# Attention and routed experts on one core: block loops written out, and three reorderings in the attention part

## What is computed

```python
# x: (2, 1024, 256), ctx: (2, 154, 256)
def attention(q_in, kv):               # 16 heads of 16
    q, k, v = q_in @ Wq + bq, kv @ Wk + bk, kv @ Wv + bv
    scores = q @ k.T / 4 - slope[h] * abs(j - i - (Nk - Nq))
    return softmax(scores) @ v @ Wo + bo
def experts(x):                        # 8 experts, 256 -> 1024 -> 256
    g = softmax(x @ Wg + bg); top2, idx = top_k(g, 2)
    top2 = top2 / (sum(top2) + 1e-8)
    return sum over e of combine[:, e] * (gelu(x @ W1[e] + b1[e]) @ W2[e] + b2[e])
x = x + attention(layernorm(x), ctx)
x = x + experts(layernorm(x))
```

## Time and profile before

| what | us |
|---|---|
| median of three runs (lowest, highest) | 479.41 (478.26, 480.38) |
| the profiled execution's own time | 479.1 |
| its span in the profile | 476.4 |
| PE, DVE, ACT, POOL busy in the span | 411.7, 314.1, 241.7, 196.7 |
| attention and routing, up to the last read of the schedule's start | 219.7 |
| blocks, from the first turned rows to the last add | 224.7 to 476.4 |

### The profile page before, as it was taken

The page is one execution under the profiler, slowest core; times in us unless marked ns, Lnnn a source line. Parts: engine busy times, 40 slices in busy tenths (PEclk is TensorE's granted clock), DMA queues, the critical chain, the costliest instruction groups (busy, mean ns, idle before and its releaser), DMA issues.

```text
span 476.4 us, 16113 instructions
## 1 busy us (share of the span) xinstructions
PE 411.7 (86%) x5037; PEld 321.7 (68%) x5038; DVE 314.1 (66%) x849; ACT 241.7 (51%) x625; POOL 196.7 (41%) x337
## 2 busy tenths in 40 slices
PE   5878898999999999931989999899989997999980
PEld 4656666666777777720867777688758876887760
DVE  6677899999988766454463666466646664666661
ACT  2337677777776556531543454345434453544430
POOL 3202488888777646683022222133212331223231
PEclk9989899999999999975898999899989998999996
DMA  7577677677776542534121331122313221322210
GB/s 262 109 193 231 196 258 216 208 196 220 220 200 205 161 111 73 162 118 147 43 50 25 48 49 35 33 44 37 45 27 56 40 44 26 51 49 29 24 14 0
DMA packets 53977, 50.70 MB, mean 106 GB/s; under 512 B 24353, under 2 KB 47905, under 8 KB 53793
## 3 DMA queue, kind: packets, MB, share of 16 engines
q1 hardware_dynamic: 46152, 41.06, 30.1%
q0 software_dynamic: 7152, 8.47, 10.5%
q10 hardware_dynamic: 624, 0.54, 0.3%
HBM read 33.73 MB, written 17.50 MB: 108 GB/s over the span
## 4 chain that ended last, share of the span: by engine, by line
PE 44%; issue 3%; DMA 3%; DVE 2%; POOL 1%; SPq 0%; ACT 0%; POOLq 0%; DVEq 0%; ACTq 0%
PE ps L1074 43%; PE ps L1310 2%; DMA out<-o,row_id 1%; DMA out<-xn,row_id 1%; DMA xlist<-rows,pos 1%; DMA area<-xlist 0%; POOL out L620 0%; DVE area L1032 0%; DVE xn L1049 0%; POOL xlist L589 0%; ACT area L775 0%; DVE o L1052 0%; DVE area L1030 0%; DVE xn L1052 0%; DVE o L1049 0%
## 5 line engine op out<-in xcount | busy, mean ns | idle before, releaser
L1074 PE MATMUL ps<-area,wts 128*128 128x128 f16 (+1 forms) x2896 | 197.6, 243 | 0.0
L1074 PEld LDWEIGHTS ps<-area,wts 128*128 (+1 forms) x2896 | 158.5, 103 | 41.2 <-issue 2.9
L1074 PE MATMUL ps<-wts,area 128*128 x624 | 154.8, 332 | 1.9 <-DVE area L1032 1.6
L775 ACT ACTIVATE area<-ps,late 128x128 f32<-128x128 f32 x312 | 89.2, 368 | 115.8 <-PE ps L1074 114.5
L1030 DVE TENSOR_SCALAR area<-area 128x512 f16<-128x512 f32 x78 | 33.0, 423 | 79.1 <-ACT area L775 79.0
L1074 PE MATMUL ps<-area 128*128 128x128 f16 (+3 forms) x832 | 66.5, 233 | 4.4 <-DMA area<-qd 2.0
L620 POOL DMA_INDIRECT out<-o,row_id x20 | 31.4, 1572 | 93.6 <-issue 64.4
L620 POOL DMA_INDIRECT out<-xn,row_id x19 | 30.1, 1587 | 94.1 <-issue 81.4
L1074 PEld LDWEIGHTS ps<-area 128*128 128x128 f16 (+1 forms) x832 | 51.0, 102 | 14.5 <-issue 6.4
L646 ACT ACTIVATE area<-ps 128x512 f32<-128x512 f32 x80 | 47.3, 595 | 24.1 <-PE ps L1074 22.3
L872 DVE TENSOR_REDUCE mx<-ps 128x3 f32<-128x462 f32 (+1 forms) x96 | 53.2, 576 | 6.9 <-PE ps L1074 6.6
(11 more groups left out here) (124 smaller groups left out, 432.0 us busy)
## 6 DMA issues: line engine op xcount, KB each, us to landing
stage<-in_w SPq DMA_DIRECT2D x32, 512.0 KB, 4.3
area<-xlist SPq DMA_DIRECT2D x39, 130.0 KB, 2.1
area<-qd SPq DMA_DIRECT2D x16, 256.0 KB, 3.6
qd<-wts SPq DMA_DIRECT2D x48, 64.0 KB, 3.1
area<-in_x SPq DMA_DIRECT2D x16, 128.0 KB, 4.6
out<-area SPq DMA_DIRECT2D x16, 128.0 KB
xlist<-pad_rows SPq DMA_DIRECT2D x11, 130.0 KB, 2.7
area<-in_b SPq DMA_DIRECT2D x1, 1024.0 KB, 6.9
```

Of the source, the lines that this page charges most:

```text
L775: last = nc.scalar.activation(h32[par][:, c * P:(c + 1) * P], h_ps[par][m][:, f * P:(f + 1) * P], ACT.Gelu_apprx_tanh, bias=b1T[:, ds(e * ...
L1074: return nc.tensor.matmul(out_, lhsT, rhs, start=start, stop=stop, skip_group_check=skip)
```

## The change

1. A new helper `straight` writes all block steps out, on all five engines. No loop and no branch is left. Expert numbers are read in longer groups: PE reads 21 values ahead of its first step and 19 between the steps t=19 and t=20; ACT reads 11 at first, then 13 ahead of t=10, 13 ahead of t=22 and 5 ahead of t=34; DVE 10, 12, 12 and 5 at the same places. SP and POOL have plain constants in their waits; the extra semaphore step that each of their waits had in a loop (`wait_alone`) goes.
2. In DVE's turn the residual and its statistics stand ahead of the rest of the turn's first weight unit, and `maxima(sc, 5)` behind the second norm's `bn_aggr`.
3. Routing's negated maximum is computed by ACT, right ahead of the exponential that uses it, no longer by POOL.
4. The rests of the last two weight units (30 and 31), which stood at the ends of turns 16 and 17, stand behind the schedule.

```diff
+        def straight(step, eng, first, ahead=None, most=NBLK):
+            t = first
+            while t < NBLK:
+                n = min(most, NBLK - t)
+                known = None if ahead is None else experts(eng, t, n + ahead)
+                for k in range(n):
+                    step(t + k, (t + k) % 4, *([] if ahead is None else [known[k:]]))
+                t += n
...
-            blocks(lambda t, slot: load_block(t + 4, slot) if not isinstance(t, int) or t + 4 < NBLK else None, sp, -4)
+            straight(lambda t, slot: load_block(t + 4, slot) if t + 4 < NBLK else None, sp, -4)
...
-            def least(t):
-                pool.wait_ge(s.m8_d, t + 1)
-                wait(pool, s.e8_d, t)
-                pool.tensor_scalar(small[:, 0:1], m8[:, 0:1], -1.0, None, ALU.mult).then_inc(s.nm_d, 1)
...
-                    least(b2)
...
-            blocks(add_block, pool, 0)
+            straight(add_block, pool, 0)
...
+                    act.wait_ge(s.m8_d, b2 + 1)
+                    wait(act, s.e8_d, b2)
+                    nc.scalar.activation(small[:, 0:1], m8[:, 0:1], ACT.Copy, scale=-1.0).then_inc(s.nm_d, 1)
                     act.wait_ge(s.nm_d, b2 + 1)
...
-            blocks(step, act, -2, 1)
+            straight(step, act, -2, 1, 12)
...
                     maxima(sc, 4)
-                for u in units[0:1] if i < NT else []:
-                    split_w_lo(u)
                 if b1 is not None:
                     dve.wait_ge(s.pr_ps, b1 + 1)
                     dve.tensor_tensor(xr[:, b1 % 8, :], misc[:, D:2 * D], xr[:, b1 % 8, :], ALU.add).then_inc(s.x2_d, 1)
                     dve.wait_ge(s.x2_d, b1 + 1)
                     dve.bn_stats(st2[:], xr[:, b1 % 8, :]).then_inc(s.st2_d, 1)
-                if sc is not None:
-                    maxima(sc, 5)
+                for u in units[0:1] if i < NT else []:
+                    split_w_lo(u)
                 if b1 is not None:
                     dve.wait_ge(s.st2_d, b1 + 1)
                     wait(dve, s.xn2_d, b1)
                     dve.bn_aggr(mv2[:], st2[:]).then_inc(s.mv2_d, 1)
                 if sc is not None:
+                    maxima(sc, 5)
+                if sc is not None:
                     negated(sc)
-                for u in earlier[1:2] + units[0:1] if i >= NT else []:
-                    split_w_lo(u)
...
             dve.tensor_copy(sched_i[0:1, 1, 0:NBLK], expert[0:1, :]).then_inc(s.sched_done, 1)
+            for u in weight_units(NT):
+                split_w_lo(u)
...
-            blocks(step, dve, -2, 0)
+            straight(step, dve, -2, 0, 12)
...
-            blocks(step, pe, -2, 1, 8)
+            straight(step, pe, -2, 1, 22)
```

## The result

The changed kernel takes 465.83 us (462.7 to 466.13, 4 runs), the kernel before 478.84 beside it (4 runs). The ratio is 0.9726, 95% interval 0.9653 to 0.9799: 2.7% faster, 13 us where 7 were forecast. The profiled execution took 465.93 (span 464.1, against 476.4).

The account below looks back on a forecast made before the run. PE was taken to bound plain block steps, with register reads idling it at loop heads; DVE and POOL paced attention turns. Terms -11.84 + 2.0 + 2.2 + 0.8 = -6.8 took 479.1 to 472.3 us, range 466.5 to 477.5.

Parts of the forecast that it names:

- Loops out: Block stage: 18.55 us of excess at PE's loop heads goes, 6.71 at t=20 comes in its place; -11.84 us.
- Longer reads on ACT and DVE: Block stage: ACT's 13-value reads ahead of t=10 and t=22 delay PE by 1.0 us each; +2.0, bounds 0 and 7.8.
- The residual ahead of the rest: Attention turns: PE's residual wait goes, but POOL's lock ends later and lengthens turns; +2.2 us, bounds -4.2 and +4.8.
- The negated maximum: Attention routing: POOL loses an operation of some 0.2 us, half-idle ACT gains 16 of 0.20; no change, 3.2 without cover.
- The last two rests: Attention's end: schedule done 1.5 us earlier, but PE's read of 21 values delays its first block; +0.8 us.
- the lower bound's case: Start of PE's first block: the load of its rows decides again, not PE's read; -1.5 us instead of +0.8.
- Plain steps of 5.53: Block steps between PE's loop heads: PE, busy throughout, bounds them, and they stay at 5.53 us.
- A: Rival, attention turns: each of eight turns gets shorter by PE's 0.53 us wait; 465.9 us, chance 0.15.
- B: Rival, blocks: the clock falls more often, at ACT's late GELUs and the long read at t=20; up to 478.1 us, chance 0.14.
- C: Rival, instruction supply: written out, each of some 33 formerly looped steps takes 0.13 us more; 476.6 us, chance 0.10.
- D: Rival: long reads cost far more per value, 0.49 us; 489 us, slower by over 0.5% from about 0.39; chance 0.05.

Follow-up runs that it names:

- The two traces compared above: First to last second norm: 157.4 us with the changed order and PE reading in groups of 12, 154.7 in the changed kernel with the residual behind the rest again.
- the run with the blocks alone: Only the written-out blocks, the three other edits undone, against the kernel before: 469.0 us, ratio 0.9715; run again on another chip, 463.45 us, ratio 0.9722.

## Why the prediction was wrong

The direction was right, the size was not: 13 us for 7. By its own steps:

- **Loops out.** The heads' 18.55 went. The price that failed is "19 x 0.242 = 4.60" plus "2.11 for the slow clock and the registers": the step measured 2.05 above 5.53, not 6.71. The read took 1.85, for it starts at number 20; every read that the trace of before had between blocks, with its start at 3, 11, 19, 27 or 35, was of the dear kind, and the one from number 0 met those of ACT and DVE, so the price per value looked constant. The clock did not fall after 1.42 us of idle time. That alone is 4.7 us of the gap. The Trainium skill's 200 ns a register, weighed there, is stated for registers loaded from the chip's main memory; these reads come from the on-chip memory, and took 0.09 a value for 19 and 21 values and 0.24 from other starts.
- **Longer reads on ACT and DVE, +2.0.** They measured 2.82 us as forecast and cost nothing. The run with those engines' loops back, ratio 0.9753, has no gain from it either. The step that failed is "A read that is 1.8 longer uses up 0.41, then 0.7; 0.7 is left for PE", with the 0.3 added for the second half. The read was 1.70 longer but began 0.13 us into PE's step, not 0.5 as at the head that I measured it at (324.5, in the step from 324.00), so the GELU came 0.8 later in the step. DVE's second split ended at 294.47 + 0.69 = 295.16, and the product that needs it started at 295.41, on time: 0.25 of the 0.81 between the two in the earlier trace rows was left.
- **The residual ahead of the rest, +2.2.** Right in its mechanism, lock included: the last second norm is 2.7 later. All seven turns from 2 to 8 are longer, by some 0.32, where I had six by 0.2; turns 13 and 14 grew by 0.45 and 0.24, where I had 0.4 and 0.5. The 2.7 itself holds some luck: the changed kernel's trace has one turn 0.8 longer with a spell of lower clock (0.50 from 98.8 to 102.2), and the trace of before a turn of 11.64 where its second one has 10.24. The two traces compared above give 2.8.
- **The negated maximum, 0.** Right: 0.9776 without it.
- **The last two rests, +0.8.** Measured at -0.7 in the changed kernel's trace. `sel` went to 0.20 as said. PE's read stands behind the rests, from 223.7 on, but takes 1.8 us and not "21 values: 5.1"; it ends at 225.5, and the load at 226.7 decides again, which was the lower bound's case. It hung on the same price of a read.
- **Plain steps of 5.53.** They are 5.65, 3.8 us over 32 steps that the sum did not have. The step that failed is "PE bounds a plain step": its products take 5.50, and its sequencer takes longer. The old 5.53 was five steps of 5.50 on a lead that the spell of lower clock had given, and two of 5.60. Of the 0.12, 0.07 is the lost lead, and the rest is fewer instructions at the slower pace of fetched code.
- **The first pass.** The 1.1 us that it took above the second went as well; the rows showed it and I left it out. In the run with PE's loop back it is 39.88 us for the seven steps of the first pass against 38.72 in the second: the pace of fetched code again, for the loop's code was fetched in its first pass only.
- **The gap.** The kernel came out at 465.93 in its profiled execution, 6.4 below the 472.3. The terms above account for 5.0 of it (4.7 + 2.0 - 0.5 + 1.5 - 3.8 + 1.1), the blocks' rows leave 0.4 open, and 0.9 lies outside the span.

The rivals: A's time, 465.9, is within 0.1 us of the result by accident, for its turns didn't get shorter. B's drops of the clock didn't come. C came, in size and in the main in kind: straight code is fetched and its sequencer is slower, though only because the sequencer already bounds the step. Its time did not come, because the price of the read fell. D asked for 0.39 us a value on the way of 66 values; the dear ones took 0.24 and cost nothing where they stood.

## What to carry to other kernels

Before a price per item is carried to a larger number, look at what else all rows of it share; here it was the start. When a stretch of slow products is removed, ask what ran ahead during it: the sequencer's lead was part of the measured plain step. Where PE is "busy" at 100% and its step still grows, count the register and wait instructions of its sequencer, and drop waits that others imply; where two engines share a lock, moving one operation can pass the lock to the next in line, as it did here.

## What the runs showed of the hardware

- A read of several values into registers costs 0.24 us a value, or, for 4 to 21 values, a third to a half of that where it starts at a value number divisible by four and no other engine reads: eleven values 1.33 against 2.65, four 0.52 against 1.01. Whether it is the address in memory that must be so aligned wasn't tried apart from the number.
- PE's sequencer issues register and wait instructions 0.124 us apart, with a longer gap at about every eighth. With these gaps it takes 0.125 on the mean in looped code that is not fetched again, and 0.131 in straight code. Some 43 of them a step made it 5.64 us where the products take 5.50; 40 left it at 5.50.
- A taken branch cost 0.22 us with a body of 8 steps and 3.37 with one of 16.
- A stop of 2.37 us lowered the clock for a while at one loop head and not at the next (6.56 against 5.14 us for the same 58 products, at 346.75 and 395.75 in the run with PE's loop back; the clock was 0.83 from the one head to the next step and 1.00 from the other). What decides stays open.
- Three reads at one moment cost more: PE's 21 values took 1.81 us alone, and 2.44 when ACT and DVE started theirs with it, in the run with the blocks alone. An overlap of two did not: where ACT's read ran beside the last 1.1 us of PE's at t=20, PE's 19 values took 1.85 as without it.
